# Last stage of a fused mixing and expert kernel: the whole residual on VectorE, four statistics buffers, smaller weight pieces, centred gating weights

## The reference, cut to what matters

```python
x = x + conv(ln(x))      # below, n = 384
# conv: xn = layer_norm(x); left, right: gated projections of xn; gate = sigmoid(xn @ Wog + bog)
out = einsum('bkjd,bkid->bijd', left, right) / n
out = layer_norm(out, on_a, on_b) * gate
out = out @ Wo + bo
# experts
t = x + ffn(ln(x))
# ffn: logits = ln(t) @ gate_w.T + gate_b; softmax over all tokens, for each of 64 experts
#      the 8 best tokens of each expert: pooled, through that expert's two layers, added back to their rows
```

## Time and profile before

| | us |
|---|---|
| median of 3 timed runs | 3089.35 (3086.25 to 3095.03) |
| the profiled execution | 3078.97 |
| its span, first to last instruction | 3077.0 |
| stage 3, about | 1883 to 2968 |

### The profile page before, as it was taken

How to read it: one execution, slowest core, us unless ns; L and a number is a source line. 1 busy time by engine, 2 the same in 40 slices (tenths; PEclk the granted TensorE clock), 3 DMA queues, 4 the chain that set the end, 5 groups by cost and what they waited for, 6 DMA issues and landing times.

```text
span 3077.0 us, 66113 instructions
## 1 busy us (share of the span) xinstructions
PE 2588.5 (84%) x14998; PEld 2145.9 (70%) x15070; DVE 2428.7 (79%) x4824; ACT 2363.5 (77%) x4284; POOL 1889.3 (61%) x2343
## 2 busy tenths in 40 slices
PE   7999999999999989989998984777777777777735
PEld 6888888888888878888988983555555555555523
DVE  6777777777777769999999996778777787787862
ACT  6888888888888877887878872888778787787850
POOL 8888888888888860000000003888788887887842
PEclk9999999999999999999999996999999999999967
DMA  5777777777777769999999985888888888888836
GB/s 199 270 267 268 267 270 273 270 269 269 267 268 268 270 256 318 333 327 325 343 330 325 332 295 185 301 309 307 297 300 309 303 299 298 309 309 297 303 139 202
DMA packets 281154, 873.00 MB, mean 284 GB/s; under 512 B 29223, under 2 KB 81602, under 8 KB 281122
## 3 DMA queue, kind: packets, MB, share of 16 engines
q1 hardware_dynamic: 272322, 855.31, 77.2%
q10 hardware_dynamic: 8448, 16.78, 1.6%
q0 software_dynamic: 352, 0.53, 0.2%
...
## 4 chain that ended last, share of the span: by engine, by line
PE 43%; DMA 17%; issue 14%; POOL 12%; DVE 5%; ACT 4%; SPq 2%; POOLq 1%; ACTq 0%; another core or an unknown queue 0%; DVEq 0%
PE banks L1267 32%; DMA arena<-left_d 11%; POOL rs L693 5%; DMA statrow<-stat_d 5%; POOL arena L664 4%; PE banks L1256 4%; PE banks L1335 3%; ACT arena L809 2%; PE banks L1301 1%; ACT work L879 1%; DVE left_parts L1006 1%; PE banks L1326 1%; PE banks L1336 1%; SPq L475 1%; DVE arena L1014 1%
## 5 line engine op out<-in xcount | busy, mean ns | idle before, releaser
L1267 PE MATMUL banks<-x_parts,w_parts 128*128 128x512 f32 x4320 | 1068.3, 399 | 0.8 <-POOL x_parts L626 0.8
L1267 PEld LDWEIGHTS banks<-x_parts,w_parts 128*128 128x128 f32 x4320 | 791.9, 189 | 162.9 <-POOL x_parts L626 1.2
L1301 PE MATMUL banks<-left_parts,right_parts 128*128 128x384 f32 x3456 | 629.3, 341 | 67.2 <-ACT arena L810 56.8
L1301 PEld LDWEIGHTS banks<-left_parts,right_parts 128*128 128x128 f32 x3456 | 606.2, 191 | 90.5 <-issue 86.0
L957 DVE SCALAR_TENSOR_TENSOR arena<-banks,cols,arena 128x512 f32<-128x512 f32 x576 | 406.6, 747 | 255.7 <-ACT arena L775 252.3
L879 ACT ACTIVATE work<-arena,nmr,rs 128x128 f32<-128x128 f32 x1152 | 458.9, 482 | 151.9 <-POOL nmr L695 145.5
L659 POOL COPY rcol<-late 128x8 f32 (+1 forms) x144 | 28.4, 197 | 722.3 <-ACT late L825 722.3
L664 POOL TENSOR_TENSOR arena<-arena,work 128x512 f32<-128x512 f32 x288 | 359.7, 1270 | 163.1 <-DVE arena L1063 161.9
L1335 PE MATMUL banks<-wo_sb,arena 128*128 128x128 f32 x2304 | 413.3, 309 | 0.1
L1335 PEld LDWEIGHTS banks<-wo_sb,arena 128*128 128x128 f32 x2304 | 373.6, 200 | 29.4 <-issue 1.8
L626 POOL TENSOR_TENSOR x_parts<-xn,x_parts 128x512 fp32r<-128x512 f32 x288 | 372.2, 1292 | 6.6 <-ACT x_parts L763 6.6
...
## 6 DMA issues: line engine op xcount, KB each, us to landing
arena<-in_x_dram SPq DMA_DIRECT2D x144, 512.0 KB, 3.4
left_d<-arena SPq DMA_DIRECT2D x144, 512.0 KB, 2.6
right_d<-arena SPq DMA_DIRECT2D x144, 512.0 KB, 3.4
gate_d<-arena SPq DMA_DIRECT2D x144, 512.0 KB, 4.2
arena<-right_d SPq DMA_DIRECT2D x128, 576.0 KB, 5.8
arena<-left_d SPq DMA_DIRECT2D x128, 576.0 KB, 6.8
mixed_d<-arena SPq DMA_DIRECT2D x128, 576.0 KB, 4.2
work<-mixed_d SPq DMA_DIRECT2D x144, 512.0 KB, 4.2
```

The costliest lines, as they stand in the source:

```text
L1267: last = nc.tensor.matmul(ps[2 + k][:, :], w_parts[:, wq, k], x_parts[:, xq, b, c], start=((wq, xq) == TERMS[0]), stop=((wq, xq) == TERMS[ ...
L1301: last = nc.tensor.matmul(ps[NT * b + t][:, 0:GRID], lr_parts[RIGHT][:, rq, b, k, t * P:(t + 1) * P], lr_parts[LEFT][:, lq, b, k], start=( ...
```

## The change

All of it but two small pieces at the start lies in stage 3.

- The residual of both halves is done on VectorE, by eight scalar_tensor_tensor in place of four. `scale_rest` on ScalarE and `residual_rest` on GpSimd go, with `s_zr` and `s_ra`; `s_r3` now counts halves.
- `statrow` has four buffers in place of two, and `load_parts` runs three steps ahead and waits for the projection four steps before. For that, SP and TensorE have loops of four steps a turn (`quads`). In a step SP now issues the rows first, then the mixed values and gate, the store and x. `exact` and its relatives move into `yt`, which is free until stage 3.
- The first weights come in halves of the 1 MB pieces, one DMA in each of 28 cuts of ScalarE's loop instead of two in each of seven; the last four follow behind the stage.
- The mean of each expert's gating weights is subtracted from them at the start. The mean of a token's row then drops out of its logits, so the normalisation needs only the scale: `minus` and `nmr` go, on VectorE and GpSimd, and `normalise` has no bias.
- `keep` copies two steps at once, every other step. The exponential's sum is written straight to `csum`, so `keep_sum` goes. On ScalarE the exponentials come first in a step.

The diff, cut to its core (declarations of buffers and semaphores and the changed counts of waits are left out):

```diff
+def quads(engine, steps, body, drain=0):
+
+    last = steps // 4 - 1
+    body(0)
+    with engine.Fori(1, last) as j:
+        body(j)
+    for j in range(last, steps // 4 + drain):
+        body(j)
...
-        statrow = sb("statrow", [P, 2, 2, CHUNK], BF16)
+        statrow = sb("statrow", [P, 4, 2, CHUNK], BF16)
...
-            def load_parts(i, b):
-                s = 2 * i + b
-                sp.wait_ge(s_z3, mark(2, s - 2, 2))
+            def load_parts(j, r):
+                s = 4 * j + r
+                if not isinstance(j, int) or j > 0:
+                    sp.wait_ge(s_z3, mark(2, s - 4, 2))
                 settle(sp, s_tick_sp)
-                sp.dma_start(statrow[0:KR, b], stat_r[s].broadcast_to([PARTS, 2 * PARTS, 2 * CHUNK])).then_inc(s_sin[b], 16)
+                sp.dma_start(statrow[0:KR, r], stat_r[s].broadcast_to([PARTS, 2 * PARTS, 2 * CHUNK])).then_inc(s_sin[r], 16)
...
             def store_result(i, b):
                 s = 2 * i + b
-                sp.wait_ge(s_r3, mark(1, s, 1))
-                sp.wait_ge(s_ra, mark(1, s, 1))
-                settle(sp, s_tick_sp)
+                sp.wait_ge(s_r3, mark(2, s, 2))
                 sp.dma_start(out[s], late_arena[:, 1, b].rearrange("p h (c d) -> p (h c) d", c=TILES)).then_inc(s_ost[b], 16)
 
-            def stage3(i):
-                for b in range(2):
-                    if in_range(i, b, 2, STEPS):
-                        load_mixed(*shifted(i, b, 2))
-                    if in_range(i, b, -1, STEPS):
-                        store_result(*shifted(i, b, -1))
-                    if in_range(i, b, 1, STEPS):
-                        load_x3(*shifted(i, b, 1))
-                    if in_range(i, b, 2, STEPS):
-                        load_parts(*shifted(i, b, 2))
+            def stage3(j):
+                for r in range(4):
+                    if in_range4(j, r, 3, STEPS):
+                        load_parts(*shifted4(j, r, 3))
+                    if in_range4(j, r, 2, STEPS):
+                        load_mixed(*halves_of(*shifted4(j, r, 2)))
+                    if in_range4(j, r, -1, STEPS):
+                        store_result(*halves_of(*shifted4(j, r, -1)))
+                    if in_range4(j, r, 1, STEPS):
+                        load_x3(*halves_of(*shifted4(j, r, 1)))
...
+            for r in range(3):
+                load_parts(0, r)
+            quads(sp, STEPS, stage3, drain=1)
...
-                pool.wait_ge(s_r3, mark(1, s - 2, 1))
-                pool.wait_ge(s_zr, mark(1, s - 2, 1))
+                pool.wait_ge(s_r3, mark(2, s - 2, 2))
                 nc.gpsimd.tensor_copy(rcol[:, b], rstd_tok[:, bass.ds(s * 2 * TILES, 2 * TILES)]).then_inc(s_rc, 1)
...
-            def residual_rest(i, b):
-                pool.wait_ge(s_x3[b], 16 * (i + 1))
-                pool.wait_ge(s_zr, mark(1, 2 * i + b, 1))
-                half = late_arena[:, 1, b, 1]
-                nc.gpsimd.tensor_tensor(half, half, wv[:, 2, b, 1], ALU.add).then_inc(s_ra, 1)
...
-            def keep(i, b):
-                s = 2 * i + b
-                pool.wait_ge(s_m3, mark(2, s, 2))
-                nc.gpsimd.tensor_copy(cand[:, bass.ds(s, 1), :], mx[:, b:b + 1, :])
-                nc.gpsimd.tensor_copy(cidx[:, bass.ds(s, 1), :], ix[:, b:b + 1, :]).then_inc(s_q3, 1)
-
-            def keep_sum(i, b):
-                s = 2 * i + b
-                pool.wait_ge(s_e3, mark(1, s, 1))
-                nc.gpsimd.tensor_copy(csum[:, bass.ds(s, 1)], esum[:, b]).then_inc(s_qs, 1)
+            def keep(i):
+                pool.wait_ge(s_m3, mark(2, 2 * i + 1, 2))
+                nc.gpsimd.tensor_copy(cand[:, bass.ds(2 * i, 2), :], mx[:, :, :])
+                nc.gpsimd.tensor_copy(cidx[:, bass.ds(2 * i, 2), :], ix[:, :, :]).then_inc(s_q3, 1)
...
-                pool.wait_ge(s_n3, mark(2, s, 1))
-                nc.gpsimd.tensor_tensor(nmr[:, b], minus[:, b], rs[:, b], ALU.mult).then_inc(s_n3, 1)
...
-                        keep(*shifted(i, b, -4))
+                        if b:
+                            keep(i - 2)
                     if in_range(i, b, -1, STEPS):
                         scales(*shifted(i, b, -1))
-                    if in_range(i, b, 0, STEPS):
-                        residual_rest(i, b)
-                    if in_range(i, b, -5, STEPS):
-                        keep_sum(*shifted(i, b, -5))
...
             def load_w1(n):
-                for j in range(2 * n, 2 * n + 2):
-                    act.dma_start(w1_sb[:, j], w1_view[j]).then_inc(s_w1, 16)
+                j, first = n // 2, BANDS // 2 * (n % 2)
+                some = slice(first, first + BANDS // 2)
+                act.dma_start(w1_sb[:, j, some], w1_view[j, :, some]).then_inc(s_w1, 16)
...
-                                     accum_out=esum[:, b]).then_inc(s_e3, 1)
-
-            def scale_rest(i, b):
-                s = 2 * i + b
-                act.wait_ge(s_rc, mark(1, s, 1))
-                act.wait_ge(s_ost[b], 16 * i)
-                act.wait_ge(s_y3, mark(2, s - 2, 2))
-                act.wait_ge(s_z3, mark(2, s, 2))
-                for c in range(TILES):
-                    last = nc.scalar.activation(summed[:, b, 1, c], ps[3][:, c * P:(c + 1) * P], ACT.Copy,
-                                                scale=rcol[:, b, TILES + c:TILES + c + 1])
-                last.then_inc(s_zr, 1)
+                                     accum_out=csum[:, bass.ds(s, 1)]).then_inc(s_e3, 1)
...
-                        last = nc.scalar.activation(ys[:, b, h, c], summed[:, b, h, c], ACT.Identity,
-                                                    bias=nmr[:, b, k:k + 1], scale=rs[:, b, k:k + 1])
+                        last = nc.scalar.activation(ys[:, b, h, c], summed[:, b, h, c], ACT.Copy, scale=rs[:, b, k:k + 1])
...
-                    if in_range(i, b, 0, STEPS):
-                        scale_rest(i, b)
+                    if in_range(i, b, -4, STEPS):
+                        exponentials(*shifted(i, b, -4))
                     if in_range(i, b, -1, STEPS):
                         normalise(*shifted(i, b, -1))
                     if in_range(i, b, -2, STEPS):
                         copy_transposed(*shifted(i, b, -2))
-                    if in_range(i, b, -4, STEPS):
-                        exponentials(*shifted(i, b, -4))
-
-            cuts = [lambda n=n: load_w1(n) for n in range(WLOADS - 1)]
+
+            cuts = [lambda n=n: load_w1(n) for n in range(4 * (WLOADS - 1))]
             pairs(act, STEPS, stage3, drain=2, cuts=cuts)
...
-            load_w1(WLOADS - 1)
+            for n in range(4 * (WLOADS - 1), 4 * WLOADS):
+                load_w1(n)
...
+            link(nc.vector.tensor_reduce(gsum[:, :], gate_nat[:, :], AXX, ALU.add))
+            link(nc.vector.tensor_scalar(gsum[:, :], gsum[:, :], 1.0 / DIM, None, ALU.mult))
+            nc.vector.tensor_scalar(gate_nat[:, :], gate_nat[:, :], gsum[:, :], None, ALU.subtract).then_inc(s_gmean, 1)
             dve.wait_ge(s_gtp, 1)
...
-                dve.wait_ge(s_z3, mark(2, s, 1))
-                for c in range(TILES):
-                    last = nc.vector.scalar_tensor_tensor(out=summed[:, b, 0, c], in0=ps[2][:, c * P:(c + 1) * P],
-                                                          scalar=rcol[:, b, c:c + 1], in1=xs[:, b, 0, c],
-                                                          op0=ALU.mult, op1=ALU.add)
-                last.then_inc(s_r3, 1)
+                for h in range(2):
+                    dve.wait_ge(s_z3, mark(2, s, h + 1))
+                    for c in range(TILES):
+                        k = TILES * h + c
+                        last = nc.vector.scalar_tensor_tensor(out=summed[:, b, h, c], in0=ps[2 + h][:, c * P:(c + 1) * P],
+                                                              scalar=rcol[:, b, k:k + 1], in1=xs[:, b, h, c],
+                                                              op0=ALU.mult, op1=ALU.add)
+                    last.then_inc(s_r3, 1)
...
-                nc.vector.tensor_scalar(over_tiles(minus[:, b]), bn[:, b, :, :, MEAN], -1.0, None, ALU.mult)
...
-                dve.wait_ge(s_q3, mark(1, s - 2, 1))
+                dve.wait_ge(s_q3, 2 + i)
...
+            pe.wait_ge(s_gmean, 1)
             nc.tensor.transpose(ps[7][:, 0:EXPERTS], gate_nat[:, :], ident[0:EXPERTS, 0:EXPERTS]).then_inc(s_gtp, 1)
...
-            def outer(i, b):
-
-                s = 2 * i + b
-                pe.wait_ge(s_sin[b], 16 * (i + 1))
+            def outer(j, r):
+                s = 4 * j + r
+                pe.wait_ge(s_sin[r], 16 * (j + 1))
                 for h in range(2):
                     pe.wait_ge(s_w3, mark(2, s - 1, h + 1))
-                    nc.tensor.matmul(ps[h][:, :], coef[:, 0, :], statrow[:, b, h, :], start=True, stop=True).then_inc(s_c3, 1)
...
                     pe.wait_ge(s_g3, mark(2, s, h + 1))
-                    pe.wait_ge((s_r3, s_zr)[h], mark(1, s - 1, 1))
```

(17 more changed lines are left out.)

65 lines of the change are left out of this document (27 added, 38 removed).

## The result

| | before | after |
|---|---|---|
| median of 4 timed runs, us | 3092.19 (3086.25 to 3099.24) | 3010.37 (3003.38 to 3025.48) |
| ratio to before, 95% interval | | 0.9741 [0.9697, 0.9785] |
| span of the profiled execution | 3077.0 | 3001.6 |
| first to last weighted product, 143 intervals | 1055.4 | 990.5 |
| that one to the last search | 29.2 | 24.3 |

The change makes the kernel 2.6% faster.

What follows compares the result with a forecast made beforehand. Loops through GpSimd and through row load and projection, 7.0 us each, plus pauses, bound the kernel. Stage 3 -59.3, start +2.7, drain -3 gave a 3017.4 us span; plus 2.0 and 10.4, 3030 us (range 3015 to 3068).

Steps and rivals of the forecast that it cites:

- the row load: Stage 3 before, later part: statistics rows' landing alternates with TensorE's projection, a loop of 7.0 us a step.
- GpSimd's loop: Stage 3 before, up to about 2540 us: gating products, power and small copies on GpSimd, 7.0 us a step.
- The memset: Kernel start: clearing the rows doubles from 1.80 us on GpSimd's serial list, adding 1.8 us.
- The 0.02 us for odd waits: Stage 3: allowance added to VectorE's 6.98 us a step, giving 7.00.
- the first steps: Start of stage 3: first three intervals take 16.1 instead of 19.8 us, step 2 waiting for mixed and gate loads.
- the drain: From last weighted product to last index search: 26.8 us instead of 29.9, gain 3 us (0 to 5).
- The pauses: Stage 3 before: seven 2 MB weight issues delay the row load, 5.0 plus about 1.5 us each, 45 us.
- Pieces: Stage 3: 28 weight transfers of 0.5 MB cost 0, as loads have 5 us to spare; uncovered, 36 us.
- Pieces and small gaps: Rival, stage 3: each piece delays a step by 1.3 us, 3066 us, or steps of 7.2, 3058; chance 0.17.
- TensorE's doubled body refetched: Rival, TensorE's stage 3 loop: code fetched again in each of 36 rounds, 65 us lost, 3095 us; chance 0.06.
- VectorE keeps its waits: Rival, stage 3: VectorE's 0.96 us of waits stay on top of 6.98, 7.94 a step, 3162 us; chance 0.08.
- The signs: Stage 3 if right: VectorE about 93% busy, products 7.0 us apart, GpSimd 63%, ScalarE 68%, clock near 1.

Runs made afterwards that it cites:

- The extra run: Changed kernel with two more scalar_tensor_tensor of 128 columns a step on VectorE, results unused: 3080.3 us, steps of 7.50 against 6.98 us.
- e14: Kernel before with only the first weights in 28 pieces of 0.5 MB instead of seven 2 MB bursts, two row buffers: 3154.76 us, ratio 1.0213.

## Where the prediction was right, and which step failed

**The mechanism was right.** The forecast named the row load and GpSimd's loop as the bounds, and VectorE as the next one at 6.98 us a step. The runs agree: four buffers alone give 0.9754, and the changed kernel's step is 6.98. Of the sum's terms, from start to start, the weighted product to the statistics measured 1.32 (1.33 summed), to the tiny operation 1.66 (1.68), that one 0.43 (0.28), eight residuals 2.08 (2.09), maximum to search 0.92 (0.91), search to product 0.60 (0.69). The two that are off, by +0.15 and -0.09, nearly cancel, which is luck. (The 6.0 that the forecast gives for VectorE's step before comes to 6.1 by the same rows; nothing hangs on it.) The extra run put 0.26 us on each residual, as the earlier trace rows had it.

**The sizes, against the profiled spans.** The forecast span was 3017.4, the measured 3001.6:

| term | forecast | measured | difference |
|---|---|---|---|
| first weighted product | 1885.6 | 1877.1 | -8.5 |
| first three intervals | 16.1 | 14.4 | -1.7 |
| 140 steps | 980.0 | 976.1 | -3.9 |
| to the last search (29.2 less 3) | 26.2 | 24.3 | -1.9 |
| the rest of the tail | 109.5 | 109.8 | +0.3 |

The sum is 15.8 us. The way from the span to the time adds 3.6: 12.4 were forecast (2.0 and 10.4), 8.8 were measured. Of the first row, stage 2's scatter is 7.4 us (678.7 against 686.1); the start itself was right, as the first projection comes 3.05 us later (2.7 forecast). The memset has its price on GpSimd's list (1.80 in the earlier trace rows):

```profile
2.58 3.51 POOL L615 MEMSET statrow<- 128x4096 bf16 x1
```

The 0.02 us for odd waits were on the safe side. So were the first steps: the forecast had step 2 wait for its loads, and it doesn't. VectorE's timeline at the first steps, where only steps 3 and 4 wait for a load (0.38 and 1.03 us), and at the last:

```profile
1877.06 1.41 DVE L1055 SCALAR_TENSOR_TENSOR arena<-work,cols,banks 128x512 f32<-128x512 f32 x2 [8.01 <-PE banks L1318]
...
1885.67 1.40 DVE L1055 SCALAR_TENSOR_TENSOR arena<-work,cols,banks 128x512 f32<-128x512 f32 x2
1891.46 1.41 DVE L1055 SCALAR_TENSOR_TENSOR arena<-work,cols,banks 128x512 f32<-128x512 f32 x2 [0.38 <-DMA work<-gate_d]
...
2867.55 1.39 DVE L1055 SCALAR_TENSOR_TENSOR arena<-work,cols,banks 128x512 f32<-128x512 f32 x2
...
2891.83 0.69 DVE L1100 FIND_INDEX8 ix<-mx,banks 128x8 uint32<-128x512 f32 x1
```

**The step that failed** is the size of the gain, which was counted from one profile of the kernel before and then carried to the median: stage 3 went into the sum as 1055.4 us, and the 10.4 us from that profiled run to the median were added whole to the changed kernel's time. For the changed kernel this difference is 7.0 us in the first comparison (3010.37 against the profiled 3003.38) and 1.7 in the second. Repeated profiles say why: before's stage 3 is 1065.9 us in the mean and was 1055.4 in the profile used, so these 10.5 us belonged to the unsteady stage that the change makes steady, and not to the part that stays. With 1065.9 in the place of 1055.4 the same sum gives 3019.3 us, inside the range and 9 us above the measured time. With the means of four and three profiles the spans differ by 83.0 us (3084.1 and 3001.1): 74.2 in stage 3, 5.2 in stage 2, where the change does nothing, 5.4 in the drain, 3 back at the start, and 1.2 in no stage of this list. Against the forecast's 59.6 that is 23.4 more, of which 10.5 are the short profile, 5.2 stage 2's scatter, 4.4 the terms of stage 3, 2.4 the drain and 0.9 small rest. The range's low end, 3015, holds a step of 6.93 (10 us) and leaves 5 us for all scatter, where stage 2 alone scatters by 14. Part of the miss is therefore chance: the time lies 4.6 us below the range, and stage 2 happened to be 7.4 us shorter after than before.

**The pauses** were put at 45 us; with the mean of the profiles stage 3 lies 65 us over steps of 7.00, 55 of them in the ten steps behind each burst: 7.8 a burst, where the forecast had 6.5. (The term doesn't enter the sum by itself, since the sum takes stage 3 as a whole.) That the cause was the small load behind the burst is shown: four buffers take the pauses away with the bursts in place.

**Pieces: right in the sum, wrong in the reason next to it.** Zero was right with four buffers. The sentence that without cover they would cost 28 x 1.3 = 36 us was too low: without it (e14) they cost 60 us more than the bursts, since a small load behind a piece lands 3.2 us later and not 1.3. The rule of the Trainium skill's "DMA: Bandwidth & Descriptors" (two cost components; rules for kernel authors), with its fixed 2.0 us (there a fit for DMAs that GpSimd issues; these are issued by ScalarE) and its 1 MiB, gave an estimate of +28 us: with four buffers the runs show none of it (3010.02 with bursts), with two more than it says (+65 us).

**The rivals.** *Pieces and small gaps*: not here, no piece moves a step. *TensorE's doubled body refetched*: the queue of instruction packets shows 7 packets in these 600 us against 3 in the earlier trace rows, far fewer than one for each of the 21 rounds (whose they are isn't shown), and TensorE's longest wait is for ScalarE's `yt`, 1.4 us. What the Trainium skill's "Runtime: NRT & Kernel Launch" (instruction fetch mechanics) says of a taken branch beyond its window isn't seen at this size of the body. The same section of the Trainium skill gives TensorE a store of 2048 instructions, which the forecast passed over. The body has 152 products and as many weight loads, so by that section it had room.

```profile
q14 instruction: 7, 0.06, 0.0%
```

*VectorE keeps its waits*: no, its three main groups have 0.7 us of idle time before them in 14 steps. The question that this rival should have raised is another: on top of four buffers, is it right to put the residual on VectorE at all? No run shows a gain from it. The forecast compared VectorE's 6.98 with the present 7.38 only, not with what the kernel would do with the old residual kept, 6.38, or 6.15 with the exponentials early (means of 120 steps in the middle).

**The signs.** VectorE 94% (93 forecast), steps of 6.98 (7.0), no step of 11 us behind a piece, clock 1.00, GpSimd 66% (63): as said. ScalarE is at 60%, not 68: the normalisation without its bias operand takes 0.29 us from start to start where it took 0.385, which the forecast counted at nothing. The chain of waits broke off in this profile, so the list of waits stands in for it.
